# A cross-attention with 64-wide heads: per-head product matrices, or q, k, V and output of two heads in one array

## What is computed

```
# L1_xattn: HEADS = 8, DIM_HEAD = 64, context ctx_1024 has 120 rows per sequence
q, k, v = x @ Wq, ctx @ Wk, ctx @ Wv               # 512 wide, 8 heads of 64
o = softmax(q_h @ k_h.T / 8) @ v_h   for each head h
x = layernorm(x + concat(o) @ Wo + bo)
# L1_ffn: ternary weights, activations rounded to 8 bits per row
xq = act_quant(x)
z  = silu(xq @ w_gate.T) * (xq @ w_up.T)           # 512 wide
x  = layernorm(x + act_quant(z) @ w_down.T)
```

## Time and profile before

| | |
|---|---|
| median of 3 runs | 2987.84 us (2985.98 to 2988.7) |
| span of the profiled execution | 3102.4 us |
| busy over the span: TensorE, VectorE, ScalarE, GpSimd | 86%, 63%, 56%, 42% |
| last stage, from its first turned input to the end | 2390.7 to 3102.4 us |
| granted TensorE clock, mean | 0.948 of full |

### The profile page before, as it was taken

How to read it: one execution, slowest core, us unless ns; L and a number is a source line. 1 busy time by engine, 2 the same in 40 slices (tenths; PEclk the granted TensorE clock), 3 DMA queues, 4 the chain that set the end, 5 groups by cost and what they waited for, 6 DMA issues and landing times. The chain is left out here.

```text
span 3102.4 us, 95215 instructions
## 1 busy us (share of the span) xinstructions
PE 2683.3 (86%) x29840; PEld 2148.4 (69%) x29967; DVE 1965.4 (63%) x5562; ACT 1745.5 (56%) x6327; POOL 1317.7 (42%) x2786
## 2 busy tenths in 40 slices
PE   5999997899999998358768969999997999999995
PEld 5899996666666665256557757777776788888884
DVE  2666664666666665333223447777775588888887
ACT  2666664455555554013335648777776566666663
POOL 0333332233333332532654446666664344444342
PEclk7999998999999999679889979999998999999997
DMA  4222222111111110112222211111111000000000
GB/s 139 72 68 74 74 74 67 32 39 36 37 38 35 38 37 21 46 49 59 62 62 61 67 45 47 46 46 46 46 46 33 21 28 23 27 23 27 23 21 11
DMA packets 252203, 143.19 MB, mean 46 GB/s; under 512 B 33568, under 2 KB 246048, under 8 KB 252064
## 3 DMA queue, kind: packets, MB, share of 16 engines
q1 hardware_dynamic: 243360, 123.45, 14.3%
q0 software_dynamic: 8704, 17.97, 1.7%
HBM read 84.41 MB, written 48.51 MB: 43 GB/s over the span
## 5 line engine op out<-in xcount | busy, mean ns | idle before, releaser
L1379 ACT ACTIVATE pr<-psS,small 128x128 f32<-128x128 f32 x1024 | 364.1, 381 | 124.3 <-DVE small L1450 101.3
L1768 ACT ACTIVATE pr<-psT 120x512 f32<-120x512 f32 (+1 forms) x512 | 278.0, 595 | 276.8 <-PE psT L1674 276.8
L1813 DVE TENSOR_REDUCE small<-psS 128x4 f32<-128x992 f32 x256 | 303.6, 1187 | 91.2 <-PE psS L1678 91.2
L1664 PE MATMUL psT<-cross_Qm,cross_xf 32*120 32x512 f32 (+1 forms) x1024 | 305.5, 639 | 34.1 <-DVE cross_xoT L1861 30.6
L937 ACT ACTIVATE pr<-psS,small 128x120 f32<-128x120 f32 x512 | 185.9, 392 | 172.7 <-DVE small L1119 172.7
L2318 POOL DMA_INDIRECT results<-experts_ob,experts_xb x144 | 138.1, 959 | 233.0 <-ACT experts_ob L2165 216.9
L1379 ACT ACTIVATION_READ_ACCUMULATOR pr<-psS,small 128x1 f32 x1024 | 223.7, 218 | 0.0
L2285 DVE SCALAR_TENSOR_TENSOR experts_bgh<-experts_bth,psS 128x256 f32<-128x256 f32 x144 | 60.7, 421 | 232.6 <-ACT experts_bth L2157 153.4
L1669 PE MATMUL psS<-cross_xf,cross_Qm 32*128 32x248 f32 x1024 | 193.1, 427 | 0.5 <-DVE small L1813 0.5
L1157 POOL TENSOR_SCALAR pr<-pr,small 128x120 f32<-128x120 f32 x512 | 178.3, 370 | 29.8 <-DVE small L1100 29.8
L1450 DVE TENSOR_REDUCE small<-psS 128x8 f32<-128x1024 f32 x128 | 156.8, 1225 | 45.1 <-PE psS L1344 42.2
(11 more groups left out here) (345 smaller groups left out, 8112.8 us busy)
## 6 DMA issues: line engine op xcount, KB each, us to landing
self_parts<-results SPq DMA_DIRECT2D x64, 192.0 KB, 2.3
slots<-blank SPq DMA_DIRECT2D x18, 520.0 KB, 4.3
experts_xb<-slots SPq DMA_DIRECT2D x144, 65.0 KB
self_near<-in_x SPq DMA_DIRECT2D x128, 64.0 KB, 1.9
between<-self_xo SPq DMA_DIRECT2D x128, 64.0 KB, 1.6
cross_x<-between SPq DMA_DIRECT2D x128, 64.0 KB, 1.8
cross_res<-between SPq DMA_DIRECT2D x128, 64.0 KB, 1.8
cross_cx<-in_ctx SPq DMA_DIRECT2D x128, 60.0 KB, 1.8
```

The source lines that it names most:

```text
L1379: last = act.activation(pr[e.slot % 4][:, cols], K.S[e.slot % 2][:, cols], ACT.Exp, bias=nmax[e.slot % 4][:, n:n + 1], accum_out=tot[k.slo ...
L1664: pe.matmul(T[0:size, 512 * n:512 * n + 512], xf[t.slot][rows(g), every][:, places[ck]], Qm[t.slot][rows(g), :], start=True, stop=False)
L1768: act.activation(PT[k][0:sizes[ck], half], T[0:sizes[ck], half], ACT.Exp).then_inc(exped, 1)
L1813: dve.tensor_reduce(out, src, AX.X, ALU.max, negate=True).then_inc(maxed, 1)
```

## The change

In place of M and N, the raw weights are kept (`K.wide`, `K.wideo`), and `set_up` loses seven of its jobs (three turns, four groups of products, and ScalarE's eviction of each). The last stage becomes `attend_pairs`. Per sequence: q and k of four head pairs, 4 products each against the turned x and context; scores in 8 products whose weights fill 64 rows, the two heads of a pair in the upper and lower half of the array and in different banks of `psS0`; V in one product of 512 columns; probabilities times V in 8 products whose weights fill 64 columns, the two heads of a pair writing partitions 0 to 63 and 64 to 127 of one bank; then 4 accumulating products with Wo. ScalarE evicts q, k, OT and V in place of two halves of xM and two of U. The turned probabilities were evicted by VectorE already, both halves, and still are. The x and the context come out of PSUM in one copy instead of two. `yb` and `fxo` move to GpSimd. The turned rounded x moves to a bank of its own. z is rounded, turned and multiplied one step later (c-6), and the hardware loop starts at step 16.

```diff
-    K.Mcross = K.sb("Mcross", [P, WH * P])
-    K.Ncross = K.sb("Ncross", [P, WH * P])
+    K.wide = K.sb("wide", [P, 3, 4 * P])
+    K.wideo = K.sb("wideo", [P, 4, P])
...
-            (stage2[:, 0, :], D["L1_xattn_Wq"]), (stage2[:, 1, :], D["L1_xattn_Wk"]), (stage2[:, 2, :], D["L1_xattn_Wv"]),
-            (wo2[:], D["L1_xattn_Wo"].rearrange("(b e) n -> e b n", e=P)),
...
-            cross_products.append(([(cols(j), wT2[row, 0, cols(j)], wT2[row, 1, cols(j)], True, True) for j in range(4)],
-                                   wide(K.Mcross)))
-            cross_products.append(([(cols(j), wT2[row, 2, cols(j)], wo2[row, j, :], True, True) for j in range(4)],
-                                   wide(K.Ncross)))
...
-        MEANS = len(turns + products + cross_turns)
-        jobs = turns + products + cross_turns + means + cross_products + ternary_turns
+        MEANS = len(turns + products)
+        jobs = turns + products + means + ternary_turns
...
+def attend_pairs(K, D, tag, x_dram, out_dram, nseq):
...
+        def place(j, half):
...
+            return (4 * half + j) * P
...
+                    a, m, b, t, n, f, r = c + 3, c + 1, c, c - 3, c - 4, c - 5, c - 6
                     if t.live:
                         need(pe, weighed, t.done(2))
...
+                            need(pe, V_sb, (c - 1).done())
+                        need(pe, O_sb, (t - 1).done())
                         for half in range(2):
+                            for j in range(J):
+                                last = pe.transpose([W0, W1][half][0:CTX, cols(j)],
+                                                    pr[t.slot][:, place(j, half):place(j, half) + P][:, 0:CTX], K.ident[:])
                             last.then_inc(pT_ps, 1)
                     if m.live:
+                        need(pe, in_sb, (c + 2).done() if (c + 2).live else m.done())
+                        if f.live:
+                            need(pe, xqT_sb, f.done())
+                        for j in range(J):
+                            last = pe.matmul(W2[:, cols(j)], wq[:, cols(j)], xc[m.slot][:, 0:P], start=True, stop=True)
+                        last.then_inc(proj_ps, 1)
+                        need(pe, summed, n.done())
+                        need(pe, fsummed, (c - 7).done())
+                        for j in range(J):
+                            last = pe.matmul(W3[:, CTX * j:CTX * j + CTX], wk[:, cols(j)], xc[m.slot][:, cT],
+                                             start=True, stop=True)
+                        last.then_inc(proj_ps, 1)
+                    if r.live:
+                        need(pe, zround, r.done(ZR))
+                        for j in range(4):
+                            last = pe.transpose(S1[:, cols(j)], zr[:, cols(j)], K.ident[:])
+                        last.then_inc(zqT_ps, 1)
+                    if b.live:
+                        need(pe, qk_sb, b.done(2))
+                        need(pe, exped, (b - 1).done(2))
+                        for j in range(J):
+                            for half in range(2):
+                                last = pe.matmul(S0[:, place(j, half):place(j, half) + CTX],
+                                                 qT[b.slot % 2][rows(half), cols(j)],
+                                                 kT[b.slot % 2][rows(half), CTX * j:CTX * j + CTX], start=True, stop=True)
+                                if j == J - 1:
+                                    last.then_inc(S_ps, 1)
+                    if t.live:
+                        need(pe, pT_sb[0], t.done())
+                        need(pe, pT_sb[1], t.done())
+                        for j in range(J):
+                            for half in range(2):
+                                h = 2 * j + half
+                                last = pe.matmul(W1[rows(half), cols(j)], V[t.slot][0:CTX, DH * h:DH * h + DH],
+                                                 pT[t.slot % 2][0:CTX, place(j, half):place(j, half) + P],
                                                  start=True, stop=True)
+                                if j == J - 1:
+                                    last.then_inc(O_ps, 1)
+                    if f.live:
+                        need(pe, xqT_sb, f.done())
+                        need(pe, zqT_sb, r.done())
+                        pe.matmul(S1[:, 0:INNER], xqT[:], K.tg[:], start=True, stop=True)
+                        pe.matmul(S1[:, INNER:], xqT[:], K.tu[:], start=True, stop=True).then_inc(gu_ps, 1)
                     if b.live:
+                        need(pe, pT_sb[0], t.done())
+                        pe.matmul(W0[0:CTX, :], xc[b.slot][:, cT], wv, start=True, stop=True).then_inc(V_ps, 1)
+                    if m.live:
+                        need(pe, qk_sb, m.done(2, 1))
...
+                    if n.live:
+                        need(pe, xround, n.done(XR))
+                        pe.transpose(W2[:, turned_x], xr[n.slot % 2][:], K.ident[:]).then_inc(xqT_ps, 1)
+                    if a.live:
+                        need(pe, x_in[a.slot], a.landed())
...
+                        pe.transpose(W2[:, 0:P], x[a.slot][:], K.ident[:])
+                        pe.transpose(W2[:, cT], cx[a.slot][0:CTX, :], K.ident[0:CTX, 0:CTX]).then_inc(in_ps, 1)
+                    if m.live:
+                        need(pe, qk_sb, m.done(2))
...
+                        need(pe, summed, n.done())
+                    if r.live:
...
+                            need(pe, fsummed, (c - 7).done())
+                        need(pe, zqT_sb, r.done())
+                        for j in range(4):
+                            last = pe.matmul(W3[:, P:2 * P], zqT[:, cols(j)], K.td[:, j, :], start=(j == 0), stop=(j == 3))
+                        last.then_inc(fout_ps, 1)
                     if t.live:
+                        need(pe, O_sb, t.done())
+                        for j in range(J):
+                            last = pe.matmul(W3[:, 0:P], OT[t.slot % 2][:, cols(j)], wo[:, j, :], start=(j == 0), stop=(j == J - 1))
+                        last.then_inc(out_ps, 1)
...
+                        need(act, S_ps, (m - 2).done(2))
+                        need(act, proj_ps, m.done(2, 1))
+                        act.activation(qT[m.slot % 2][:], W2[:], ACT.Copy, scale=gain).then_inc(qk_sb, 1)
+                        need(act, proj_ps, m.done(2))
+                        act.copy(kT[m.slot % 2][:], W3[:, 0:J * CTX]).then_inc(qk_sb, 1)
+                    if r.live:
+                        need(act, zqT_ps, r.done())
+                        need(act, fout_ps, (r - 1).done())
+                        act.activation(zqT[:], S1[:, 0:INNER], ACT.Identity, bias=K.unround[:]).then_inc(zqT_sb, 1)
+                    if t.live:
+                        need(act, O_ps, t.done(2))
+                        need(act, out_ps, (t - 2).done())
+                        act.copy(OT[t.slot % 2][:], W1[:]).then_inc(O_sb, 1)
                     if f.live:
                         need(act, gu_ps, f.done())
                         need(act, zround, (f - 1).done(ZR))
+                        act.activation(th[:], S1[:, 0:INNER], ACT.Tanh, scale=big[f.slot][:, 3:4]).then_inc(tanhed, 1)
+                    exps(b, range(0, 2))
                     if b.live:
...
+                        dve.tensor_copy(xc[a.slot][:], W2[:, 0:P + CTX]).then_inc(in_sb, 1)
...
+                        need(pool, inverted, w.done())
+                    if o.live:
+                        pool.tensor_tensor(frs[o.slot % 2][:], fve[o.slot % 2][:], K.half[:, 0:1], ALU.pow).then_inc(flnroot, 1)
                     if w.live:
                         weigh(w, 0)
+                    if o.live:
+                        need(pool, flnroot, o.done())
+                        need(pool, stored[o.slot], (o - 4).landed())
+                    if t.live:
+                        need(pool, res_in[t.slot], t.landed())
+                        need(pool, summed, (t - 2).done())
+                        pool.tensor_tensor(yb[t.slot % 2][:], res[t.slot][:], K.rowb[:, 2, :], ALU.add).then_inc(joined, 1)
+                    if o.live:
+                        pool.tensor_scalar(fxo[o.slot][:], fy[o.slot % 2][:], fmv[o.slot % 2][:, 0:1], frs[o.slot % 2][:, 0:1],
+                                           ALU.subtract, ALU.mult).then_inc(fnormed, 1)
```

More of the change, by code:

```diff
@@ L685, in attend_window @@
         K.passed()
-def attend_wide(K, D, tag, x_dram, out_dram, nseq, windowed, last_pass=False):
+def attend_pairs(K, D, tag, x_dram, out_dram, nseq):
     nc = K.nc
     ring = 4
-    keys = P if windowed else CTX
-    M, N = (K.Mself, K.Nself) if windowed else (K.Mcross, K.Ncross)
-    early = 6 if windowed else 8
-    last_gain = P ** -0.5 if windowed else 64 ** -0.5
-    feed = not windowed
-    scores = K.S if windowed else [K.S[0], K.S[0]]
+    J, DH = 4, 64
+    gain = DH ** -0.5
+    inner = J * P
+    wq, wk, wv = (K.wide[:, n, :] for n in range(3))
+    wo = K.wideo
```

(68 more changed lines are left out.)

491 lines of the change are left out of this document (146 added, 345 removed).

## The result

| | before | after |
|---|---|---|
| median of 4 runs, us | 2986.91 (2985.31 to 2988.7) | 2892.37 (2891.38 to 2894.35) |
| span of the profiled execution, us | 3102.4 | 2892.6 |
| last stage, from its first load of x to the end, us | 713.5 | 617.8 |
| first to fifth score maxima, us | 35.4 | 25.3 |
| 58 steady steps, us (one) | 594.03 (10.24) | 510.62 (8.80) |

The ratio is 0.9684, with a 95% interval of 0.9672 to 0.9696: 94.5 us less, where 90 were forecast. All of it is in the last stage, which is 95.7 us shorter.

The account below looks back on a forecast made before the run. A loop through TensorE, ScalarE and VectorE was taken to bound the step at 10.24 us. A new step of 8.8 gives 83.5, plus 2.5 in set_up and 4 at the ends: 90 off 2987.8, 2898 us, range 2870 to 2940.

Parts of the forecast that it names:

- The bound: Last stage before: a loop through TensorE, ScalarE and VectorE closes the step at 10.23 us, not TensorE alone.
- The pair overlap: Last stage, TensorE: paired scores take 1.09 us for 1.77, paired V products 1.10 for 1.89.
- The change of shape: TensorE's array changes shape three times per step, 0.09 us each; the pitches used already hold two of the three.
- The loop: New step: q, k, z, scores, V products, then ScalarE's work to the turned x's eviction, sum 8.73 us, taken as 8.8.
- the tie I assumed: Before tanh: gate and up finish at the same time as the OT copy, 0.44 + 0.19 against 0.66 us.
- three bounds: New step: loop 8.73, TensorE 8.1, VectorE 8.4 us plus waits; near-equal bounds rarely give the largest alone, so 8.8.
- VectorE and GpSimd: Per step: VectorE falls from 9.0 to 8.4 us busy; GpSimd rises from 4.1 to 5.4, narrowly hidden.
- the rival in which VectorE closes the step: Last stage: VectorE's waits add up, step 9.0 to 9.5 us, 2926 us; chance 0.18, shared with GpSimd as bound.
- V products alone: Last stage: only V products fail to overlap, 1.89 us for 1.10, step 9.6, 2944 us; chance 0.08.
- no pair: Last stage: neither scores nor V products overlap, step 10.27 us, 2983 us, no change; chance 0.04.
- The ends: Filling and emptying the last stage's pipeline, some dozen steps: gain 0 to 17 us, taken as 4.
- set_up: Seven jobs before the ternary turns go: gain bounded by 0 to 2.9 us, taken as 2.5.

Follow-up runs that it names:

- e7: V product over 128 columns in place of 512, leaving out three quarters of V, against the changed kernel: 3003.1 us (3098.0 before beside it), 8.80 us per step.
- e6: Eviction of the turned x two exponentials earlier on ScalarE, against the changed kernel: 2982.5 us (3098.0 before beside it), 8.38 us per step.
- e9: Full-size tiles for scores and V products, heads not separated, against the changed kernel: 3096.9 us (3098.0 before beside it), 10.18 us per step.
- e1: Score products ordered by halves, so neighbours don't alternate, against the changed kernel: 2933.8 us (2987.9 before beside it), 9.34 us per step.
- e2: V products ordered by halves, so neighbours don't alternate, against the changed kernel: 2925.1 us (2987.9 before beside it), 9.28 us per step.
- e3: Scores and V products both ordered by halves, without alternation, against the changed kernel: 2961.1 us (2987.9 before beside it), 9.82 us per step.
- e4: `yb` and `fxo` put back on VectorE, against the changed kernel: 2908.3 us (2987.9 before beside it), 9.00 us per step.
- e12: The changed kernel unaltered, run again on a slower chip: 3002.3 us (3095.5 for the kernel before beside it), 8.80 us per step.

## Why the prediction was right, point by point

**The bound.** "No plain TensorE bound, and work taken off TensorE counts only as far as it or its order is in a loop": shown by e7, 0.64 us off TensorE for 0.00 us of step, and by e6, no work removed and 0.42 us less.

**The pair overlap.** Scores were put at 1.09 and measured 1.09; V products at 1.10 (0.94 to 1.16) and measured 1.02, from their start to that of gate and up. The neighbouring rows of another stage were the right source for both, row strips and column strips. The gains were put at 0.68 and 0.79; with full tiles in the same order (e9) the two groups take 1.78 and 1.79, so they are 0.69 and 0.77. The second came close by two errors: the output products before were priced by their columns at 1.89, while their own row gives 1.95 - 0.17 = 1.78, and the V products at 1.10 for 1.02. Nor is the gain all alternation: 0.54 and 0.48 are alternation (e1, e2), the rest, 0.36 of the step after the 0.09 for the change of shape, is that a half is cheaper than a full tile (e9 against e3). The rule cited from the Trainium skill, "TensorE: Matmul & The Clock Gate", Part 3, by which only a different row group lets a weight load overlap, would have made e2 equal to the change; it was 0.48 us a step longer. For column halves the measurement decides against the rule.

**The change of shape.** 0.09 was forecast from the earlier trace rows; 0.53 against 0.44 before the scores (after and e9) shows 0.09. The Trainium skill's drain at a change of tiling mode ("TensorEngine Tiling (Array Packing)", Key Properties) is no more than that at this place.

**The loop.** Term by term 8.73 was forecast and 8.85 stands in the step shown. z turned is 0.09 longer, since I had that change of shape in the pitches already; the OT copy blocks 0.58 and not 0.47, because tanh follows gate and up, which end 0.11 later than the tie I assumed; q's release is 0.10 later; V products with their run-out are 0.13 shorter. The mean of 58 steps is 8.80, exactly the value used, and that is partly luck: these errors cancel in part, and what they leave is about the 0.07 that was added because three bounds lay close. No such effect shows: TensorE waits for the eviction before q in each of the 58 steps, so this loop alone gives the time. The first q product is released by the eviction of the turned x, as said.

**VectorE and GpSimd.** VectorE's busy time came out lower than forecast: 7.8 us a step (88.64 x 8.80 / 100), not 8.4, so "over 90 of 100" did not show. The price of the two operations on GpSimd was right: `yb` 0.46 and `fxo` 0.80, and they hide. The weighing ends at 2607.80, and TensorE takes it up at 2608.31 behind the products with Wo. The loop of the rival in which VectorE closes the step exists, as in "the turning of z now needs VectorE early in the same step as tanh feeds it late", but at 8.38 and not 9.0 to 9.5 it isn't the bound of the changed kernel. It is with the two operations still on VectorE (e4).

**No overlap.** By their conditions these two rivals are e2 (V products alone, forecast 9.6 a step and 2944 us) and e3 (no pair, 10.27 and 2983). Measured were 9.28 and 9.82 a step, 2925.1 and 2961.1 us: both rivals took a half without overlap to cost as much as a full tile. The price of 10.27 and no change belongs to e9, which measured 10.18 and a ratio of 0.9995. So without the halves nothing is left of the gain.

**The ends.** This term was mis-sized: 4 us taken of 0 to 17, and 12.3 measured (first load to first maxima 0.94, next four steps 10.14, tail 1.21). "One sequence's chain sets the pace" there, and that chain got shorter: its steps last 5.9 to 6.9 us in place of 7.9 to 9.5. Filling alone would be 6.4 us shorter with full tiles too (e9, 29.05 against 35.43 us from first to fifth maxima), by the new order. But e9 loses 5.9 us again from the 63rd maxima to the end (74.3 against 68.4), and e3 5.8 (74.1). So at the two ends together the new order without the overlap gives little; the pairs are needed there as well.

**set_up.** 2.5 us was forecast; the first turned input comes at 45.79 us, 1.6 earlier than the 47.42 before. The first ternary turns did start 4 us earlier than in the earlier trace rows, at 37.11, more than the 2.9 allowed for, as VectorE too had their input 1.1 us earlier. But then a load of SyncE, issued 0.8 us earlier than before and landing 5.2 us later in place of 4.3, stands in front of the next stage's first load:

```profile
37.11 1.97 PE L341 MATMUL psT<-ident,ternq 128*128 128x128 f32 x8 [4.21 <-DVE tstep L323]
37.44 1.43 SPq L268 DMA_DIRECT2D blank<-in_c_spare  x1
...
43.09 1.77 SPq L434 DMA_DIRECT2D self_x<-in_x  x4
```

Even that is lost later: the first indirect DMA for `slots` is at 1267.58 us in the profile after and at 1265.44 before. This term was worth nothing. So the sum reads 83.4 + 12.3 and about -1, against 83.5 + 4 + 2.5: the loop, which is most of it, was right, and the two small terms missed in opposite directions.

**The long span of the profile.** Its 114.6 us over the median were rightly kept out of the forecast. They lie in the expert stage, which the change doesn't touch: its writes of `results` start at 1435.9 and end at 1800.5 us in that profile, as in e12. The two rows below are the stretch from 1250 to 1700 us of the changed kernel in its first profile and in e12: the granted TensorE clock is 0.94 and 0.82 of full in the mean, DMA moves 73 and 57 GB/s. Which of the two comes first the rows don't tell, and it was not tested.

```profile
1250.00:1700.00 450.00, 365.51 (x2092) 295.72 (x2092) 196.37 (x429) 205.91 (x609) 264.63 (x281) 0.94 0.26 73
```

```profile
1250.00:1700.00 450.00, 308.37 (x1576) 245.50 (x1575) 155.98 (x333) 136.58 (x418) 214.73 (x226) 0.82 0.21 57
```

## What to carry to other kernels

Price a new order as a loop, and write down the second and the third loop too: here three of them (8.80 over ScalarE, 8.38 over VectorE, TensorE's own work close to that) lay within 0.5 us, and each later edit met the next one. Where heads are 64 wide, let neighbouring products alternate between halves of the array; the same products in the order of the halves gave back 67.8 of the 94.5 us (e3). And a small eviction that frees a shared PSUM bank should stand as early on its engine as its input allows: two exponentials behind it instead of ahead were worth 22 us.

## What the runs showed of the hardware beyond that

- A float32 record of 120 or 128 columns takes 0.111 or 0.112 us in a full tile (e9), 0.101 with 64 rows and 0.095 with 64 weight columns when its neighbour uses the same half, and 0.068 or 0.064 when it uses the other (e3 and the change). A float32 product is two records, so two products in different halves take 0.26 to 0.27 us together, one alone in its half 0.19 to 0.20: they overlap only in part.
- One kernel on two chips: the same last stage to 0.01 us in 510, and 110 us of difference in one stage with indirect DMA (e12).
